# Value projection of a window-attention kernel: three rounded passes of 128 columns over a split operand instead of one fp32 product per tile

## The reference

```python
x = x + L0(group_norm(x))   # attention inside windows of 8 x 8 pixels, 8 heads of 16 channels
x = x + L1(group_norm(x))   # linear attention over the image, depthwise conv, MLP of 1024

# L0, per window of 64 tokens
xn = layer_norm(win) * ln_gamma + ln_beta
qkv = xn @ w_qkv.T + b_qkv
q, k, v = split(qkv)        # then softmax(q k^T / 4) v per head, and the output projection
```

## Time and profile before

| | us |
|---|---|
| median of 3 runs | 2759.55 (2758.84 to 2760.31) |
| profiled execution, its time | 2760.2 |
| its span, first to last instruction | 2758.4 |
| TensorE busy (share of the span) | 2589.6 (94%) |
| VectorE busy | 2266.0 (82%) |
| ScalarE busy | 2134.6 (77%) |
| GpSimd busy | 1368.3 (50%) |
| mean granted TensorE clock | 0.985 of full speed |

### The profile page before, as it was taken

The page is one execution under the profiler, slowest core; times in us unless marked ns, Lnnn a source line. Parts: engine busy times, 40 slices in busy tenths (PEclk is TensorE's granted clock), DMA queues, the critical chain, the costliest instruction groups (busy, mean ns, idle before and its releaser), DMA issues.

```text
span 2758.4 us, 89023 instructions
## 1 busy us (share of the span) xinstructions
PE 2589.6 (94%) x34410; PEld 2131.3 (77%) x34410; DVE 2266.0 (82%) x5003; ACT 2134.6 (77%) x3921; POOL 1368.3 (50%) x1322
## 2 busy tenths in 40 slices
PE   2999899989999999899979999999999999999999
PEld 2777677767777777799958888888888888888887
DVE  5888788888887888577788888888888888888885
ACT  2777677767777777455569999999999999999997
POOL 1555455545555555345524555555555555555454
PEclk9999999999999999899989999999999999999999
DMA  4222122222221111233301101111111011100000
GB/s 138 75 69 72 55 88 80 67 64 81 72 73 43 53 53 41 88 100 114 113 14 41 40 30 41 41 41 37 40 41 38 34 40 40 41 24 20 20 20 21
DMA packets 55773, 151.83 MB, mean 55 GB/s; under 512 B 6609, under 2 KB 20945, under 8 KB 55633
## 3 DMA queue, kind: packets, MB, share of 16 engines
q1 hardware_dynamic: 55632, 149.93, 16.9%
HBM read 98.52 MB, written 51.38 MB: 54 GB/s over the span
## 4 chain that ended last, share of the span: by engine, by line
PE 85%; DVE 6%; ACT 5%; issue 3%; DMA 1%; POOL 1%; DVEq 0%; SPq 0%; POOLq 0%; ACTq 0%
PE bank L1255 14%; PE bank L1257 14%; PE bank L1256 14%; PE bank L1487 12%; PE bank L1320 7%; PE bank L1309 5%; PE bank L1408 5%; ACT prob L663 4%; PE bank L1416 3%; PE bank L1334 3%; DVE vx L933 3%; PE bank L1272 2%; PE bank L1244 2%; PE bank L1304 1%; DMA ximg<-x_in 1%
## 5 line engine op out<-in xcount | busy, mean ns | idle before, releaser
L598 POOL TENSOR_TENSOR hl<-hf,hh 128x448 fp32r<-128x448 f32 x448 | 517.7, 1156 | 637.8 <-ACT hh L791 637.8
L1139 DVE SCALAR_TENSOR_TENSOR bank<-oring,dw,bank 128x448 f32<-128x448 f32 x896 | 614.9, 686 | 20.1
L1487 PE MATMUL bank<-hw,w 128*128 128x448 f32 x896 | 391.2, 538 | 0.0
L1255 PE MATMUL bank<-t1h,w_hi 128*128 128x448 f32 x896 | 365.0, 407 | 6.0 <-DVE t1l L1156 6.0
L788 ACT ACTIVATE hf<-bank,fc1b 128x448 f32<-128x448 f32 x448 | 282.6, 631 | 111.7 <-PE bank L1257 111.7
L1257 PE MATMUL bank<-t1l,w_hi 128*128 128x448 f32 x896 | 325.7, 364 | 0.0
L1256 PE MATMUL bank<-t1h,w_lo 128*128 128x448 f32 x896 | 323.1, 361 | 0.0
L1320 PEld LDWEIGHTS bank<-vx,prob 128*64 128x64 f32 x6272 | 202.9, 139 | 100.9 <-issue 83.3
L791 ACT ACTIVATE hh<-hf 128x448 fp32r<-128x448 f32 x448 | 259.2, 579 | 14.2
L782 ACT ACTIVATE hw<-bank,fc1b 128x448 f32<-128x448 f32 x448 | 265.9, 618 | 0.4 <-PE bank L1257 0.4
L940 DVE TENSOR_REDUCE mx<-bank 128x8 bf16<-128x512 f32 x448 | 248.4, 617 | 10.2 <-PE bank L1289 7.4
(11 more groups left out here) (156 smaller groups left out, 6810.8 us busy)
## 6 DMA issues: line engine op xcount, KB each, us to landing
ximg<-x SPq DMA_DIRECT2D x112, 448.0 KB, 3.4
ximg<-x_in SPq DMA_DIRECT2D x56, 448.0 KB, 3.4
x<-ximg SPq DMA_DIRECT2D x56, 448.0 KB, 2.5
y_out<-yb SPq DMA_DIRECT2D x112, 224.0 KB, 1.9
xs<-x_in SPq DMA_DIRECT2D x42, 448.0 KB, 3.4
wm<-wm_in SPq DMA_DIRECT2D x1, 512.0 KB, 4.1
w1f<-w_in SPq DMA_DIRECT2D x1, 512.0 KB, 5.3
w<-w_in SPq DMA_DIRECT2D x1, 512.0 KB, 7.4
```

The source lines that it names most:

```text
L598: g.tensor_tensor(hl[:, k, :], hf[:, k % 2, :], hh[:, k, :].bitcast(F32), ALU.subtract).then_inc(hl_ready, 1)
L1139: m = d.scalar_tensor_tensor(acc, src, dw[:, k:k + 1], acc, ALU.mult, ALU.add)
L1255: mm(out, w[0], x[0], start=start, stop=False)
L1487: m = mm(out, w2[:, j, :], hw[:, WHOLE_J.index(j), :], start=first, stop=last)
```

## The change

The split weights `pws` grow from two matrices (q, k) to three (q, k, v); ScalarE rounds and VectorE subtracts 384 columns instead of 256. `project_v` issues three accumulating fp32r passes per tile, high tokens by high weights, high tokens by low weights, low tokens by high weights, instead of one fp32 product of `xn` and `wv`. Stationary operand (the tokens) and streamed columns (128) keep their shapes. No wait is added or moved.

```diff
--- before.py
+++ after.py
@@ -93,7 +93,7 @@
         w2 = sb("w2", [P, NF, P])
         w2s = [sb(f"w2_{n}", [P, NS, P], F32R) for n in ("hi", "lo")]
         lws = [sb(f"lw_{n}", [P, 4, P], F32R) for n in ("hi", "lo")]
-        pws = [sb(f"pw_{n}", [P, 2, P], F32R) for n in ("hi", "lo")]
+        pws = [sb(f"pw_{n}", [P, 3, P], F32R) for n in ("hi", "lo")]
         ctxs = [sb(f"ctx_{n}", [P, NIMG, P], F32R) for n in ("hi", "lo")]
         ident16 = sb("ident16", [P, P], BF16)
         neghalf = sb("neghalf", [P, 4])
@@ -608,7 +608,7 @@
         def _(act):
             a = nc.scalar
             act.wait_ge(consts_loaded, 16 * NCONST)
-            a.activation(pws[0][:], wm[:, 0:2, :], ACT.Copy)
+            a.activation(pws[0][:], wm[:, 0:3, :], ACT.Copy)
             a.activation(lws[0][:], wm[:, WMATS.index("lwq"):WMATS.index("lwq") + 4, :], ACT.Copy)\
                 .then_inc(weights_hi, 1)
             act.wait_ge(par_ready, 1)
@@ -860,7 +860,7 @@
             d.scalar_tensor_tensor(par_("K2"), v("bfc2"), par_("s2"), par_("B2"), ALU.mult, ALU.add)\
                 .then_inc(par_ready, 1)
             dve.wait_ge(weights_hi, 1)
-            d.tensor_tensor(pws[1][:], wm[:, 0:2, :], pws[0][:].bitcast(F32), ALU.subtract)
+            d.tensor_tensor(pws[1][:], wm[:, 0:3, :], pws[0][:].bitcast(F32), ALU.subtract)
             d.tensor_tensor(lws[1][:], wm[:, WMATS.index("lwq"):WMATS.index("lwq") + 4, :],
                             lws[0][:].bitcast(F32), ALU.subtract).then_inc(weights_lo, 1)
             dve.wait_ge(par_ready, 1)
@@ -1269,7 +1269,8 @@
             def project_v(G, gg):
                 for t in range(GROUP_PAIRS[gg]):
                     c = slice(P * t, P * t + P)
-                    m = mm(bank[7][:, c], xn[:, gg, c], wmat("wv"), start=True, stop=True)
+                    for k, (x, w) in enumerate(((xns[0], pws[0]), (xns[0], pws[1]), (xns[1], pws[0]))):
+                        m = mm(bank[7][:, c], x[:, gg, c], w[:, 2, :], start=(k == 0), stop=(k == 2))
                 m.then_inc(v_mm, 1)
 
             def quad_rows(j):
```

## The result

The changed kernel took 2788.47 us (median of 4 runs, 2782.59 to 2801.43) against 2759.93 us before (median of 4): a ratio of 1.0107, 95% interval 1.0075 to 1.0140, 28.5 us slower. The forecast was 2788.5 us. The profiled execution was one of the shorter ones: 2785.63 us, span 2783.8, granted clock 0.988.

The account below looks back on a forecast made before the run. The prediction took the chain of waits through the window-attention stage as the bound, no engine being solid. It added 21.8 and 7.3 us, 29.1 in all, to the median of 2759.55, giving 2788.5 us, range 2776 to 2799.

Parts of the forecast that it names:

- The slot: Spacing of rounded value-projection passes on TensorE: 111 ns, set by the weight load, with 120 ns as upper end.
- a fast load: Rival, chance 0.05: rounded loads go at the bf16 rate, slot 57 ns, 14.5 us back, 2745 us.
- a slow narrow pass: Rival, chance 0.06: each rounded pass of 128 columns takes 222 ns, 157 us more, 2917 us.
- the tail: Fixed time added to the slots of a set of value-projection passes: 220 ns for rounded passes.
- Four tiles: Four-tile value projections, ahead of VectorE's copies on the chain: 0.39 us longer each, 56 times, 21.8 us.
- Three tiles: Three-tile value projections, 0.28 us longer: through VectorE's queue they delay project_q by 0.22 us in 33 strips, 7.3 us.
- the slack of 0.06 us on oh: Three-tile half: room between VectorE's end of oh, plus a 0.05 us signal, and project_q's first load; subtracted from 0.28 us.
- The sum: Attention stage: 21.8 us for four-tile plus 7.3 us for three-tile projections, 29.1 us more in all.
- Edits that cost nothing: Splitting 384 weight columns instead of 256, once beside the first loads: under 0.49 us even uncovered; no DMA or wait added.
- The granted clock of the attention stage: Sign of a wrong forecast: TensorE's granted clock, 0.99 before, falling in that stage with the shorter streams.

Follow-up runs that it names:

- stream64: The changed kernel with only 64 of the 128 weight columns streamed in each of the three passes: ratio 1.0145 to the kernel before.
- load64: The changed kernel with only 64 of the 128 tokens of a tile loaded in each pass: ratio 0.9974 to the kernel before.
- bf16: The changed kernel with the value projection's three passes on bf16 operands, low bits left out: ratio 0.9961 to the kernel before.
- four_only: The changed kernel with the three rounded passes only in four-tile groups, three-tile groups keeping the fp32 product: ratio 1.0073 to the kernel before.
- stats_moved: The changed kernel with the moments of the next image's strip moved from behind the three-tile copies to ahead of the four-tile copies: ratio 1.0090 to the kernel before.
- reorder_before: The kernel before with attend 0 and out_project ahead of the wait on v_ready, attend 1 and ln_transpose behind it: ratio 1.0185 to the kernel before.
- again: The unchanged changed kernel run and profiled a second time, beside the other experiments: ratio 1.0120 to the kernel before.

## Why the prediction was right

- *The slot.* Forecast 111 ns because the load sets it. Measured 111 to 112 ns, and shown by stream64, load64 and bf16 to be the load's. The rivals of a fast load and of a slow narrow pass are out. The records last 275 ns and not the 220 forecast. A record starts inside its own load (a record at 825.73, its load from 825.68 to 825.87), which may be why; no run tests it. The sets of twelve and nine took 1.55 and 1.22 us all the same, so the tail was right as a term of the set.
- *Four tiles.* 56 x 0.39 = 21.8 us forecast. The strip of four_only is 0.40 longer in all images, 22.4 us if all 56 strips do as those in the middle, and they do so only roughly; its runs give 1.0073, or 20.1 us (15.7 to 24.6) on 2758.92.
- *Three tiles.* The path through copies, moments, maxima and oh is right, as stats_moved shows. The size was off: 0.22 us forecast, 0.28 measured. The term that was mis-sized is the slack of 0.06 us on oh: I took a signal from VectorE to cost 0.05 us, from the copies to L1320, but from the end of oh to the load of project_q it is 0.12 in the changed kernel (841.67, 841.79) and in reorder_before (833.60, 833.72), and 815.87 - 815.75 = 0.12 in the earlier trace rows too. There was no slack at all. So the term is 33 x 0.28 = 9.2 us instead of 7.3.
- *The sum.* 29.1 us forecast, about 22.4 + 9.2 = 31.6 by the measured strips, 28.5 by the first four runs, and 34.9 in the group of again (2793.77 against 2758.92). Runs with the same mean clock bring these together: at 0.985 that group has two of each kernel, 2790.93 us on average against 2759.90, 31.0 us apart. The interval of the first, 1.0075 to 1.0140, is 21 to 39 us. So the strips' 31 us is the better figure, the forecast was 2 us short of it for the missing slack, and that the first median met 2788.5 within 0.1 us is luck.
- *Edits that cost nothing.* The block stage kept its length (1339.8 us), no transfer grew (151.8 MB in both). The weights' split was not measured by itself; the first loads of the score products (L1289, L1290 after) started at 58.8 us against 57.6, and in again at 57.8.
- *What the forecast had not:* that the lower clock level at the images' heads would spread the times. Before, the runs of one group spread too (2754.0 to 2767.59). The granted clock of the attention stage, named as a sign of being wrong, stayed 0.99 in the first profile and was 0.97 in again (50 to 1155 us). That the change lowers it is not shown: the mean clocks of the runs in that group were 0.982 to 0.985, and 0.981 to 0.988 before.

## What to carry to other kernels

Price a pass of TensorE by the larger of its load and its stream: at 128 columns each rounded pass costs a whole load of a four-byte operand, and two-byte operands halved it here. Look for cover on every engine behind an instruction, not only on its own: the three-tile set had 0.65 us of idle behind it on TensorE and still cost 0.28, because VectorE's queue had no gap between reading its result and the next thing that TensorE waits for.

## What I had not expected of the hardware

A signal took about 0.05 us from the end of VectorE's copies to the start of L1320, but 0.12 us from the end of its product oh to a load of L1255, in three kernels; what makes the difference is open. With bf16 operands, passes of 512 columns follow each other at 0.216 us instead of 0.23, though neither type's load (98 and 192 ns) is as long as either. Why is open.
